# The ternary forms of the third window's gate and up move from VectorE to GpSimd, the opening begins in another order, and the third window's pairs are added in two steps

## The chip, the cores and the metric

One core of a Trainium2 chip runs the kernel. Its engines are TensorE (PE; PEld is its weight load), VectorE (DVE), ScalarE (ACT), GpSimd (POOL) and SyncE (SP), which issues most DMAs. The metric is the device time of one execution in microseconds (us), lower is better.

## The reference, cut to what matters

A batch of 32 sequences of 64 channels by 1024 features is first mixed over its channels (64x64 weights picked by an index of each sequence), then goes through a feed-forward layer whose weights are octonions quantized to -1, 0, 1 times a scale, and is added to the input.

```python
def ternary_dequant(W):
    scale = jnp.mean(jnp.abs(W))
    return scale * jnp.clip(jnp.round(W / scale), -1.0, 1.0)

def oct_ternary_linear(xp, W):          # xp: (..., 8, d)
    M = jnp.einsum('jik,jod->koid', S_OCT, ternary_dequant(W))
    return jnp.einsum('...id,koid->...ko', xp, M)

y = jnp.einsum('bct,bcd->bdt', x, cond_w[itok])
gate = oct_ternary_linear(y, w_gate); up = oct_ternary_linear(y, w_up)   # 8 x 341 hidden
h = silu(gate) * up
out = x + oct_ternary_linear(h, w_down)
```

## The kernel before, in words

The 2048 tokens are worked on in 8 tiles (T = 0 to 7) of 256. The 341 hidden rows of each octonion part are cut into three windows: two of 128 rows and a last one, "the third", of 85 (`THIRD`, `LAST`). In each tile 12 chunks c follow one another, four to a window; a chunk gives two of the eight parts of h. Chunks 0 to 7 belong to the two full windows, 8 to 11 to the third. A "down" stage ends the tile: `h` and sums of `h` (six rounds k = 0 to 5 of `z`, two to a window) are multiplied by the down weights.

Each engine has its own program, written out by hand; engines meet only at semaphores, and an engine runs its instructions in the order in which they are written. For a chunk PE makes sums in PSUM from the weight tables (`shared_pair`, `shared`, `own`), DVE adds the shared part, ACT takes the silu, DVE multiplies, ACT copies the result twice (`split_h`), DVE writes the low half (`h_lo`). PE may begin `own` of chunk c only when `h_lo` of chunk c - 2 is done.

**The opening.** Before the first product the weights' mean magnitudes must be known: ACT sums magnitudes (`sum_abs`), PE adds them over the partitions, DVE makes scale and half scale of them (`scales(m)`, m = 0 gate, 1 up, 2 down). DVE then makes the ternary form of a window in two instructions, a comparison at L919 and a comparison minus the first at L921 (`ternary`), and builds half of the table from it (`build_table`, four sums at L895); ACT copies or negates the rest (`copy_slots`). The activations y come as high and low half: `y_hi` on ACT, `y_lo` on DVE, in three pieces. PE starts chunk 0 when two pieces of `y_lo` are there, and its up half when the up table is.

**Tile 0.** Only window 0 of gate and up is made in the opening, and window 1 of gate. The rest stands between the chunks of tile 0 on DVE: `TERN_AFTER` and `TABLE_AFTER` say after which chunk a ternary form or a table (matrix, window) comes, `DOWN_AFTER` the same for the three windows of the down weights. After chunk 5 DVE makes the scales of tile 1 (`scales_of_tile(1)`). After chunk 6's `own`, PE begins to mix the down weights of the third (`mix`, L1201), which waits for the down weights' last ternary form and for the first of those scales. On GpSimd the sums of y (`sum_y(0)`) come first, then the mixing of the down weights' two full windows (`mix_down_weights`), and then five of the six rounds of z.

**A round of z** (`round_of_z`, GpSimd) waits for the four chunks of its window, adds pairs of h (`pair_up`, two or four instructions), and then adds and subtracts the pairs (two instructions). ACT writes the high half (`z_hi`), DVE the low half (`z_lo`). Round 5 is DVE's own (`last_round_of_z`). In the last tile ACT and DVE take round 5 before round 4:

```python
def last_rounds(T):
    ks = range(NR - 2, NR)
    return ks if T + 1 < NT else ks[::-1]
```

## Time and profile before

| | |
|---|---|
| median of 3 runs | 679.83 us (679.83 to 680.08) |
| the profiled execution | 679.09 us, its span 677.3 us |
| PE busy | 643.8 us (95% of the span) |
| PEld busy | 595.5 us (88%) |
| DVE busy | 516.5 us (76%) |
| POOL busy | 385.1 us (57%) |
| ACT busy | 323.2 us (48%) |
| mean TensorE clock granted | 0.986 |

Shares are of the whole span; the opening and tile 0 (the first 122 us) and the last tile look unlike the six tiles between. A matmul's end is modelled, so a PE that is shown busy can still be slow; its clock stands in a column of its own.

### The profile page before, as it was taken

How to read it: one execution, taken by the hardware profiler on the slowest of the kernel's cores; microseconds unless marked ns; L12 is line 12 of the kernel's file. 1: busy time of each engine (PE TensorE's matmuls, PEld its weight loads, DVE VectorE, ACT ScalarE, POOL GpSimd, SP SyncE). 2: the span in 40 equal slices, each digit the busy share in tenths (PEclk: the TensorE clock that was granted, in tenths of full speed). 3: DMA queues.
4: the chain of work that ended last, by engine and by line, in shares of the span. 5: the costliest groups of instructions: out<-in, count | busy, mean ns of one | idle time of the engine just before them, and what ended most of it. 6: DMA issues, size and time to landing. Idle time of an engine off the chain costs nothing. (4 is left out here: it accounts for less than half of the span.)

```text
span 677.3 us, 17118 instructions
## 1 busy us (share of the span) xinstructions
PE 643.8 (95%) x7010; PEld 595.5 (88%) x7010; DVE 516.5 (76%) x873; ACT 323.2 (48%) x542; POOL 385.1 (57%) x453
## 2 busy tenths in 40 slices
PE   3599899999999999999999999999999999999997
PEld 3378699899999999998998999999999999988986
DVE  1899977868776787868877698767878687787785
ACT  4847455345534545254454446254462545434440
POOL 1256685547637576348646476376754486465553
PEclk9799899999999999999999999999999999999997
DMA  9200030140003200041001300031000300021001
GB/s 345 67 2 1 1 116 15 39 155 1 2 2 102 90 2 2 1 137 55 2 2 61 132 1 2 1 126 68 1 2 6 121 1 2 2 72 55 2 1 63
DMA packets 10576, 31.50 MB, mean 47 GB/s; under 512 B 3330, under 2 KB 3330, under 8 KB 10370
## 3 DMA queue, kind: packets, MB, share of 16 engines
q1 hardware_dynamic: 9906, 28.81, 12.3%
q10 hardware_dynamic: 592, 1.61, 0.7%
q8 instruction: 55, 0.90, 0.6%
q14 instruction: 23, 0.19, 0.1%
HBM read 22.02 MB, written 8.39 MB: 45 GB/s over the span
## 5 line engine op out<-in xcount | busy, mean ns | idle before, releaser
L1240 PE MATMUL ps<-y_op,gate_table 128*128 128x256 f16 x1408 | 182.6, 275 | 8.2 <-DVE y_op L979 4.2
L1240 PE MATMUL ps<-y_op,up_table 128*128 128x256 f16 x1408 | 180.3, 273 | 0.2 <-ACT up_table L724 0.2
L1240 PEld LDWEIGHTS ps<-y_op,gate_table 128*128 128x128 f16 x1408 | 138.3, 99 | 27.3 <-issue 4.4
L1240 PEld LDWEIGHTS ps<-y_op,up_table 128*128 128x128 f16 x1408 | 137.9, 98 | 16.8 <-DVE up_table L895 0.7
L617 POOL TENSOR_TENSOR h_pairs<-h_f 128x256 f32<-128x256 f32 (+2 forms) x128 | 118.0, 949 | 60.0 <-ACT h_f L767 57.7
L524 POOL TENSOR_TENSOR o_sb<-o_sb,wd_sb 128x256 f32<-128x256 f32 (+1 forms) x150 | 87.4, 617 | 90.8 <-DVE wd_sb L1108 89.6
L617 POOL TENSOR_TENSOR z_f<-h_pairs 128x512 f32<-128x512 f32 (+1 forms) x80 | 103.7, 1317 | 43.0 <-DVE z_op L995 41.2
L1248 PE MATMUL ps<-third_table,y_op 128*128 128x170 f16 x1408 | 108.2, 237 | 0.6 <-ACT third_table L724 0.6
L1248 PEld LDWEIGHTS ps<-third_table,y_op 128*128 128x128 f16 x1408 | 105.1, 97 | 1.1 <-issue 0.8
L822 ACT ACTIVATE ps<-ps,small 128x512 f32<-128x512 f32 x64 | 42.4, 662 | 111.0 <-DVE ps L1009 85.0
L1401 PE MATMUL ps<-down_u,z_op 128*128 128x256 f16 (+1 forms) x768 | 92.8, 277 | 2.0 <-DVE z_op L995 2.0
L1401 PE MATMUL ps<-down_c,h_op 128*128 128x128 f16 (+1 forms) x1536 | 92.8, 220 | 0.0
L895 DVE TENSOR_TENSOR pu_sb<-ps,q_sb 128x170 f32<-128x170 f32 (+1 forms) x128 | 64.9, 507 | 33.9 <-PE ps L1240 14.1
L1401 PEld LDWEIGHTS ps<-down_c,h_op 128*128 128x128 f16 (+1 forms) x1536 | 89.6, 98 | 0.7
L1401 PEld LDWEIGHTS ps<-down_u,z_op 128*128 128x128 f16 (+1 forms) x768 | 75.0, 99 | 11.4 <-DVE z_op L995 2.1
L988 DVE TENSOR_TENSOR h_op<-ps,h_op 128x512 f16<-128x512 f32 (+1 forms) x96 | 65.8, 685 | 21.8 <-ACT h_f L767 21.8
L995 DVE TENSOR_TENSOR z_op<-z_f,z_op 128x1024 f16<-128x1024 f32 (+1 forms) x40 | 49.5, 1237 | 34.1 <-ACT z_op L782 34.1
L762 ACT ACTIVATE h_op<-ps 128x512 f16<-128x512 f32 (+1 forms) x96 | 57.3, 597 | 31.4 <-DVE ps L1083 30.6
L767 ACT ACTIVATE h_f<-ps 128x512 f32<-128x512 f32 (+1 forms) x96 | 57.6, 600 | 0.0
L782 ACT ACTIVATE z_op<-z_f 128x1024 f16<-128x1024 f32 (+1 forms) x40 | 42.1, 1053 | 32.2 <-POOL z_f L617 32.2
L1083 DVE SCALAR_TENSOR_TENSOR ps<-pu_sb,small,ps 128x512 f32<-128x512 f32 x64 | 48.3, 755 | 8.1 <-ACT ps L822 2.0
L1009 DVE TENSOR_TENSOR pu_sb<-ps,pu_sb 128x512 f32<-128x512 f32 x48 | 32.9, 686 | 19.4 <-PE ps L1240 19.4
(98 smaller groups left out, 643.2 us busy)
## 6 DMA issues: line engine op xcount, KB each, us to landing
x_in<-in_x_dram SPq DMA_DIRECT2D x8, 1024.0 KB, 5.1
o_sb<-in_x_dram SPq DMA_DIRECT2D x16, 512.0 KB, 3.7
out_dram<-o_sb SPq DMA_DIRECT2D x15, 512.0 KB, 2.7
h_op<-in_L_ffn_w_gate_dram ACTq DMA_DIRECT2D x3, 512.0 KB, 6.8
h_op<-in_L_ffn_w_up_dram SPq DMA_DIRECT2D x3, 512.0 KB, 7.4
z_op<-in_L_ffn_w_down_dram SPq DMA_DIRECT2D x1, 1536.0 KB, 11.4
out_dram<-o_sb SPq DMA_DIRECT2D x2, 256.0 KB, 2.2
cond_bd<-in_L_cond_weights_dram SPq DMA_DIRECT2D x30, 16.0 KB, 3.0
```

The source lines that it names most:

```text
L524: last = eng.tensor_tensor(dst, dst, wd_sb[:, s, k1, r0, h, :], ALU.add if sign > 0 else ALU.subtract)
L617: return pool.tensor_tensor(dst, a, b, ALU.add if sign > 0 else ALU.subtract)
L762: act.activation(h_op[rows, c, :, 0, :], h_bank(c), ACT.Copy).then_inc(h_hi_ready, 1)
L767: act.activation(h_f[rows, c], h_bank(c), ACT.Copy).then_inc(h_copied, 1)
L822: act.activation(bank_r(s, 0), bank_r(s, 0), ACT.Silu, scale=gate_scale(T)).then_inc(silu_ready, 1)
L895: return dve.tensor_tensor(dst, a, b, ALU.add if sign > 0 else ALU.subtract)
L988: dve.tensor_tensor(h_op[rows, c, :, 1, :], h_bank(c), h_op[rows, c, :, 0, :], ALU.subtract).then_inc(h_lo_ready, 1)
L995: dve.tensor_tensor(z_op[rows, k, 1], z_of(k), z_op[rows, k, 0], ALU.subtract).then_inc(z_lo_ready, 1)
L1083: dve.scalar_tensor_tensor(out=bank_r(s, 0), in0=u_sb[:], scalar=up_scale(T), in1=bank_r(s, 0), op0=ALU.mult, op1=ALU.mult).then_inc(h_rea ...
L1240: mm = pe.matmul(dst, table[m][:, slot, q, :], y_op[:, op, e, :], start=(i == 0 and e == 0), stop=(i == len(terms) - 1 and e == 1))
L1248: mm = pe.matmul(dst, y_op[:, op, e, P * s:P * s + P], third_table[:, slot].rearrange("p m r -> p (m r)"), start=(i == 0 and e == 0), stop ...
L1401: mm = pe.matmul(banks[bank][:, place], operand[:, P * s:P * s + P], weights, start=(bank not in begun), stop=(last and i == ends[bank]), ...
```

## The change: what it does

Three edits. **The opening**: PE adds the gate's magnitudes after the first of the four rounds of y instead of after the second; DVE sums the magnitudes of two of up's windows instead of one, before the scales of y instead of after them; ACT sums one window instead of two, and copies its half of the up table before it sums the down weights; DVE's `h_scales(0)` moves behind the third piece of `y_lo`. **The third's ternary forms**: GpSimd makes them, in three instructions each (two comparisons and a subtraction, 128 x 8 x 85 elements), after the up table of window 0 is built and before it mixes the down weights; the readers wait for a semaphore of GpSimd's. DVE no longer makes them, and builds the third's gate table after chunk 4 instead of 5. **The third's pairs**: in every tile round 4 adds the pairs of chunks 8 and 9 as soon as these are there, those of chunks 10 and 11 later.

The diff, cut to its core:

```diff
-    TERN_AFTER = {1: (1, 1), 4: (0, 2), 6: (1, 2)}
-    TABLE_AFTER = {0: (0, 1), 2: (1, 1), 5: (0, 2), 6: (1, 2)}
+    TERN_AFTER = {1: (1, 1)}
+    TABLE_AFTER = {0: (0, 1), 2: (1, 1), 4: (0, 2), 6: (1, 2)}
...
+        def wait_for_tern(engine, m, w):
+
+            if w == THIRD:
+                engine.wait_ge(third_tern_ready, m + 1)
+            else:
+                engine.wait_ge(tern_ready[m], w + 1)
...
-        def pair_up(add, k, pairs):
+        def pair_up(add, k, pairs, parts=(0, 1)):
...
-                a_runs = [(slice(0, 2), signs[0])] if signs[0] == signs[1] else [
-                    (slice(a, a + 1), signs[a]) for a in range(2)]
+                a_runs = [(slice(0, 2), signs[0])] if signs[0] == signs[1] and len(parts) == 2 else [
+                    (slice(a, a + 1), signs[a]) for a in parts]
...
+            def ternary_of_third(m):
+                raw_at, dst = [ap[m][THIRD][:, :, 0:LAST] for ap in (raw, tern)]
+                above = pairs_of_down[:, 0:2].rearrange("p n j o -> p (n j) o")[:, :, 0:LAST]
+                pool.wait_ge(scale_ready, 3 * (m + 1))
+                if m > 0:
+                    pool.wait_ge(third_tern_ready, m)
+                pool.tensor_scalar(above, raw_at, half[m], None, ALU.is_gt).then_inc(third_compared, 1)
+                pool.tensor_scalar(dst, raw_at, minus_half[m], None, ALU.is_lt).then_inc(third_compared, 1)
+                pool.wait_ge(third_compared, 2 * m + 2)
+                pool.tensor_tensor(dst, above, dst, ALU.subtract).then_inc(third_tern_ready, 1)
...
             def round_of_z(T, k):
                 n = (NR - 1) * T + k
-                pool.wait_ge(h_copied, NC * T + 4 * (k // 2) + 4)
-                if n > 0:
+                if k == NR - 2:
+
+                    pool.wait_ge(h_copied, NC * T + NC - 2)
                     pool.wait_ge(z_ready, n)
-                pair_up(signed_add, k, h_pairs).then_inc(pairs_ready, 1)
+                    pair_up(signed_add, k, h_pairs, (0,))
+                    pool.wait_ge(h_copied, NC * T + NC)
+                    pair_up(signed_add, k, h_pairs, (1,)).then_inc(pairs_ready, 1)
...
                 if T == 0:
+
+                    pool.wait_ge(slots_built[1], NBUILD)
+                    ternary_of_third(0)
+                    ternary_of_third(1)
                     mix_down_weights(0)
                     mix_down_weights(1)
...
-            for w in range(NQ - 1):
-                sum_abs_of(1, w)
+            sum_abs_of(1, 0)
             y_hi(0)
+            copy_slots(1, 0)
             act.wait_ge(down_loaded, 16)
-            sum_abs(2 * NQ - 1, raw_down_at, NQ * raw_n, abs_sum[2])
-            copy_slots(1, 0)
+            sum_abs(NQ + 1, raw_down_at, NQ * raw_n, abs_sum[2])
...
             build_table(0, 0)
+            for w in range(1, NQ):
+                dve.wait_ge(up_loaded[w], 16)
+                dve.tensor_reduce(abs_sum[1][:, w:w + 1], raw[1][w].rearrange("p j o -> p (j o)"), AX.X, ALU.add,
+                                  apply_absolute_value=True).then_inc(abs_summed_dve, 1)
             y_scales(0)
...
             scales_of_ffn()
-            h_scales(0)
             y_lo(0, range(2))
             ternary_of(1, 0)
             build_table(1, 0)
             y_lo(0, range(2, NY))
+            h_scales(0)
             ternary_of(0, 1)
...
-            for r in range(2):
-                y_round(0, r)
+            y_round(0, 0)
             sum_abs(0)
-            for r in range(2, 4):
+            for r in range(1, 4):
                 y_round(0, r)
             row_norms(0)
```

How the instructions stand now. First DVE in the opening, from the last piece of the gate table (before: from the last scale of y) to the first pieces of `y_lo`; L1123 (after: L1156) is the sum of magnitudes, L945 to L954 (L978 to L987) the scales of y, L901 and L905 (L934, L938) `scales(1)`, L959 to L967 `h_scales(0)`. Before:

```order
L954 TENSOR_SCALAR small<-small 128x1
L1123 TENSOR_REDUCE small<-h_op 128x1
L901 TENSOR_REDUCE small<-ps 128x1
L905 TENSOR_SCALAR small<-small 128x1 x3
L909 TENSOR_SCALAR small<-small 128x1
L911 TENSOR_SCALAR small<-small 128x1
L959 TENSOR_SCALAR small<-small 128x1
L962 TENSOR_SCALAR small<-small 128x1
L965 RECIPROCAL small<-small 128x1
L967 TENSOR_SCALAR small<-small 128x1
L979 SCALAR_TENSOR_TENSOR y_op<-y_f,small,y_op 128x4x256 x2
```

After:

```order
L928 TENSOR_TENSOR gate_table<-z_op 128x2x128 x2
L1156 TENSOR_REDUCE small<-h_op 128x1 x2
L978 TENSOR_REDUCE small<-ps 128x1
L980 TENSOR_SCALAR small<-small 128x1
L983 TENSOR_SCALAR small<-small 128x1
L986 RECIPROCAL small<-small 128x1
L987 TENSOR_SCALAR small<-small 128x1
L934 TENSOR_REDUCE small<-ps 128x1
L938 TENSOR_SCALAR small<-small 128x1 x3
L942 TENSOR_SCALAR small<-small 128x1
L944 TENSOR_SCALAR small<-small 128x1
L1012 SCALAR_TENSOR_TENSOR y_op<-y_f,small,y_op 128x4x256 x2
```

The two sums now stand ahead of the scales of y, and the four instructions of `h_scales(0)` are gone from here.

Second GpSimd between `sum_y(0)` and the mixing of the down weights (`wd_sb<-o_sb` are that mixing's pairs). Before:

```order
L617 TENSOR_TENSOR y_f<-y_f 128x256 x2
L617 TENSOR_TENSOR y_f<-y_f 128x512
L617 TENSOR_TENSOR y_f<-y_f 128x256 x2
L617 TENSOR_TENSOR wd_sb<-o_sb 128x512 x2
L617 TENSOR_TENSOR wd_sb<-o_sb 128x384
```

After:

```order
L626 TENSOR_TENSOR y_f<-y_f 128x256 x2
L661 TENSOR_SCALAR wd_sb<-h_op,small 128x8x85
L662 TENSOR_SCALAR z_op<-h_op,small 128x8x85
L664 TENSOR_TENSOR z_op<-wd_sb,z_op 128x8x85
L661 TENSOR_SCALAR wd_sb<-h_op,small 128x8x85
L662 TENSOR_SCALAR z_op<-h_op,small 128x8x85
L664 TENSOR_TENSOR z_op<-wd_sb,z_op 128x8x85
L626 TENSOR_TENSOR wd_sb<-o_sb 128x512 x2
L626 TENSOR_TENSOR wd_sb<-o_sb 128x384
```

Six instructions of 680 elements a partition have come in.

Third DVE from the end of chunk 4 to the down weights' last ternary form (`o_sb<-z_op`). Before:

```order
L1083 SCALAR_TENSOR_TENSOR ps<-pu_sb,small,ps 128x512
L919 TENSOR_SCALAR z_op<-h_op,small 128x8x85
L921 SCALAR_TENSOR_TENSOR z_op<-h_op,small,z_op 128x8x85
L895 TENSOR_TENSOR pu_sb<-ps,q_sb 128x512
L988 TENSOR_TENSOR h_op<-ps,h_op 128x2x256
L895 TENSOR_TENSOR ps<-ps,pu_sb 128x256 x2
L895 TENSOR_TENSOR pu_sb<-ps,pu_sb 128x256 x2
L1083 SCALAR_TENSOR_TENSOR ps<-pu_sb,small,ps 128x512
L895 TENSOR_TENSOR third_table<-z_op 128x4x85 x2
L895 TENSOR_TENSOR third_table<-z_op 128x2x85 x2
L919 TENSOR_SCALAR o_sb<-z_op,small 128x1024
L921 SCALAR_TENSOR_TENSOR o_sb<-z_op,small,o_sb 128x1024
```

After:

```order
L1116 SCALAR_TENSOR_TENSOR ps<-pu_sb,small,ps 128x512
L928 TENSOR_TENSOR third_table<-z_op 128x4x85 x2
L928 TENSOR_TENSOR third_table<-z_op 128x2x85 x2
L928 TENSOR_TENSOR pu_sb<-ps,q_sb 128x512
L1021 TENSOR_TENSOR h_op<-ps,h_op 128x2x256
L928 TENSOR_TENSOR ps<-ps,pu_sb 128x256 x2
L928 TENSOR_TENSOR pu_sb<-ps,pu_sb 128x256 x2
L1116 SCALAR_TENSOR_TENSOR ps<-pu_sb,small,ps 128x512
L952 TENSOR_SCALAR o_sb<-z_op,small 128x1024
L954 SCALAR_TENSOR_TENSOR o_sb<-z_op,small,o_sb 128x1024
```

The gate's two ternary instructions of the third are gone, and its table stands where they stood, so that chunk 5 is followed at once by the down weights' ternary form.

## Rows read from the trace of the kernel before

**Rows 1.** The page: TensorE's busy time, share of the span, instructions

```profile
PE 643.8 (95%) x7010; PEld 595.5 (88%) x7010; DVE 516.5 (76%) x873; ACT 323.2 (48%) x542; POOL 385.1 (57%) x453
```

**Rows 2.** Busy time by stretch: stretch, its length, each engine's, PEclk, DMA share, GB/s

```profile
202.00:640.00 438.00, 437.01 (x4781) 406.31 (x4779) 336.65 (x567) 205.59 (x337) 259.46 (x306) 1.00 0.12 41
```

**Rows 3.** PE's timeline: start, us busy, instructions [idle before <-releaser]

```profile
27.18 3.60 PE L1240 MATMUL ps<-y_op,gate_table 128*128 128x256 f16 x16 [4.21 <-DVE y_op L979]
...
69.86 1.91 PE L1240 MATMUL ps<-y_op,up_table 128*128 128x256 f16 x16
74.48 0.33 PE L1201 MATMUL ps<-o_sb,ident 128*128 128x128 f16 x3 [2.71 <-DVE small L945]
...
661.48 6.38 PE L1401 MATMUL ps<-down_u,z_op 85*128 85x256 f16 x32 [1.95 <-DVE z_op L995]
```

**Rows 4.** DVE's timeline, opening and chunk 0

```profile
20.23 0.42 DVE L945 TENSOR_REDUCE small<-ps 128x1 f32<-128x256 f32 x1 [1.35 <-PE ps L1234]
...
21.26 1.21 DVE L1123 TENSOR_REDUCE small<-h_op 128x1 f32<-128x1024 f32 x1
...
24.65 2.47 DVE L979 SCALAR_TENSOR_TENSOR y_op<-y_f,small,y_op 128x1024 f16<-128x1024 f32 x2
...
30.22 1.81 DVE L979 SCALAR_TENSOR_TENSOR y_op<-y_f,small,y_op 128x1536 f16<-128x1536 f32 x1
31.95 0.75 DVE L919 TENSOR_SCALAR z_op<-h_op,small 128x1024 f16<-128x1024 f32 x1
32.73 1.28 DVE L921 SCALAR_TENSOR_TENSOR z_op<-h_op,small,z_op 128x1024 f16<-128x1024 f32 x1
34.77 0.69 DVE L895 TENSOR_TENSOR pu_sb<-ps,q_sb 128x512 f32<-128x512 f32 x1 [0.76 <-PE ps L1240]
...
38.28 1.15 DVE L895 TENSOR_TENSOR gate_table<-z_op 128x512 f16<-128x512 f16 x4
...
41.33 0.68 DVE L895 TENSOR_TENSOR pu_sb<-ps,q_sb 128x512 f32<-128x512 f32 x1
```

**Rows 5.** DVE's timeline, chunks 5 to 7 of tile 0

```profile
68.09 2.57 DVE L895 TENSOR_TENSOR third_table<-z_op 128x340 f16<-128x340 f16 x4
...
80.72 0.90 DVE L895 TENSOR_TENSOR third_table<-z_op 128x340 f16<-128x340 f16 x4
81.54 1.22 DVE L995 TENSOR_TENSOR z_op<-z_f,z_op 128x1024 f16<-128x1024 f32 x1
```

**Rows 6.** ACT's timeline: first pieces of y, round 0 of z, round 5 of tile 7

```profile
21.37 2.19 ACT L746 ACTIVATE y_op<-y_f,small 128x1024 f16<-128x1024 f32 x2
...
79.78 1.06 ACT L782 ACTIVATE z_op<-z_f 128x1024 f16<-128x1024 f32 x1
...
656.74 1.06 ACT L782 ACTIVATE z_op<-h_f 85x1024 f16<-85x1024 f32 x1 [4.82 <-DVE h_f L895]
```

**Rows 7.** POOL's groups by shape up to 130 us: busy, mean ns | idle before

```profile
L617 POOL TENSOR_TENSOR wd_sb<-o_sb 128x512 f16<-128x512 f16 x4 | 4.5, 1154 | 24.1 <-DVE o_sb L921 24.1
...
L669 POOL TENSOR_SCALAR down_u<-down_u 128x256 f16<-128x256 f16 x2 | 1.7, 850 | 0.2
```

**Rows 8.** POOL's groups by shape, 130 to 640 us

```profile
L617 POOL TENSOR_TENSOR z_f<-h_pairs 128x512 f32<-128x512 f32 x54 | 67.4, 1269 | 31.3 <-DVE z_op L995 30.2
...
L617 POOL TENSOR_TENSOR h_pairs<-h_f 128x256 f32<-128x256 f32 x56 | 38.9, 725 | 33.0 <-ACT h_f L767 33.0
```

**Rows 9.** POOL's and DVE's timelines, end of tile 7

```profile
652.00 4.16 POOL L617 TENSOR_TENSOR h_pairs<-h_f 85x256 f32<-85x256 f32 x4 [3.10 <-ACT h_f L767]
656.24 2.83 POOL L617 TENSOR_TENSOR z_f<-h_pairs 85x512 f32<-85x512 f32 x2
...
657.83 2.32 DVE L995 TENSOR_TENSOR z_op<-h_f,z_op 85x1024 f16<-85x1024 f32 x1 [1.12 <-ACT z_op L782]
660.20 1.22 DVE L995 TENSOR_TENSOR z_op<-z_f,z_op 85x1024 f16<-85x1024 f32 x1
```

**Rows 10.** TensorE's clock around the last wait: stretch, length, PE busy, PEclk, DMA, GB/s

```profile
662.00:664.00 2.00, 2.00 (x12) 0.54 0.03 8
```

More of the change, by code:

```diff
@@ L405, in build @@
         fixed_scales = sem("fixed_scales")
+        third_compared = sem("third_compared")
+        third_tern_ready = sem("third_tern_ready")
         compared = sem("compared")
@@ L648, in mix_down_weights @@
                 pool.wait_ge(tern_ready[2], w + 1)
+                if w == 0:
+                    pool.wait_ge(third_tern_ready, 2)
                 if w > 0:
@@ L673, in round_of_z @@
                 n = (NR - 1) * T + k
-                pool.wait_ge(h_copied, NC * T + 4 * (k // 2) + 4)
-                if n > 0:
+                if k == NR - 2:
+                    pool.wait_ge(h_copied, NC * T + NC - 2)
                     pool.wait_ge(z_ready, n)
-                pair_up(signed_add, k, h_pairs).then_inc(pairs_ready, 1)
+                    pair_up(signed_add, k, h_pairs, (0,))
+                    pool.wait_ge(h_copied, NC * T + NC)
+                    pair_up(signed_add, k, h_pairs, (1,)).then_inc(pairs_ready, 1)
+                else:
+                    pool.wait_ge(h_copied, NC * T + 4 * (k // 2) + 4)
+                    if n > 0:
+                        pool.wait_ge(z_ready, n)
+                    pair_up(signed_add, k, h_pairs).then_inc(pairs_ready, 1)
                 pool.wait_ge(pairs_ready, n + 1)
@@ L757, in split_h @@
                 if T == 0 and c % 4 == 0:
-                    act.wait_ge(tern_ready[0], c // 4 + 1)
-                    act.wait_ge(tern_ready[1], c // 4 + 1)
+                    wait_for_tern(act, 0, c // 4)
+                    wait_for_tern(act, 1, c // 4)
                 rows = slice(0, ROWS[c // 4])
@@ L1120, in _ @@
             build_table(0, 0)
+            for w in range(1, NQ):
+                dve.wait_ge(up_loaded[w], 16)
+                dve.tensor_reduce(abs_sum[1][:, w:w + 1], raw[1][w].rearrange("p j o -> p (j o)"), AX.X, ALU.add,
+                                  apply_absolute_value=True).then_inc(abs_summed_dve, 1)
             y_scales(0)
-            dve.wait_ge(up_loaded[NQ - 1], 16)
-            dve.tensor_reduce(abs_sum[1][:, NQ - 1:NQ], raw[1][NQ - 1].rearrange("p j o -> p (j o)"), AX.X, ALU.add,
-                              apply_absolute_value=True).then_inc(abs_summed_dve, 1)
             scales(1)
             scales_of_ffn()
-            h_scales(0)
             y_lo(0, range(2))
@@ L1184, in sum_abs @@
             def sum_abs(m):
-                pe.wait_ge(abs_summed, (NQ, 2 * NQ - 1, 2 * NQ)[m])
                 if m == 1:
-                    pe.wait_ge(abs_summed_dve, 1)
+                    pe.wait_ge(abs_summed_dve, NQ - 1)
+                pe.wait_ge(abs_summed, NQ + m)
                 pe.matmul(totals(m), ones[:], abs_sum[m], start=True, stop=True).then_inc(totals_ready, 1)
```

4 lines of the change are left out of this document (2 added, 2 removed).

## The prediction

> **What bounds the kernel now.** I began with the page and the busy time by stretch: PE is busy for 643.8 of 677.3 us [rows 1], and from 202 to 640 us for 437.01 of 438 at full clock [rows 2]. The reader is to see that the six middle tiles have nothing to give: whatever DVE, ACT and POOL do there lies under matmuls. So only the opening, tile 0 and the end of the last tile can move the time. PE's timeline shows where it waits there [rows 3]: 4.21 us before the first product, for `y_lo` on DVE; 2.71 us at 71.77 to 74.48 before the mixing, for a scale of tile 1 that DVE comes to late; 1.95 us before 661.48, for round 4 of z. In between, DVE's timeline is nearly gapless from 27 us to the end of chunk 7: tile 0 goes at DVE's pace, and PE's waits there are what DVE leaves. I therefore follow DVE's queue.
>
> **A price that decides: DVE against GpSimd.** The four table sums of the third take 2.57 us at 68.09, while POOL works, and 0.90 at 80.72, while it is idle [rows 5]. At the end of tile 7 the row says it outright [rows 9]: DVE's `z_lo` starts at 657.83 and takes 2.32 us, the next one 1.22. POOL's last z instruction ends at 656.24 + 2.83 = 659.07, and 659.07 + 1.22 = 660.29, which is within 0.15 us of the slow one's end. So a DVE instruction of this kind doesn't run slower beside POOL, it waits until POOL's instruction is over, and POOL waits in turn. I take that for the comparisons, for table sums and for `y_lo`; the chunk's own additions, which read PSUM, are 0.68 to 0.69 us wherever they stand [rows 4] and I let them run free.
>
> **What POOL's new instructions cost.** Six of 680 elements a partition. Two-input f32 instructions give 725 ns for 256 and 1269 for 512 elements [rows 8]: 2.13 ns an element and 0.18 us fixed. The subtraction is f16; 512 elements are 1154 ns [rows 7], so (1154 - 180)/512 = 1.9 ns an element, 1.47 us for 680. For a comparison the nearest row is the one scalar operation, 850 ns for 256 [rows 7]: with 0.18 fixed, 2.62 ns an element, 1.96 us. The bounds: 0.9 us, if one input costs half of two an element (0.18 + 680 x 1.06 ns); 2.26 us, if the 850 ns are all slope. I take 1.96, by the row of its own kind. The sum is 4 x 1.96 + 2 x 1.47 = 10.8 us.
>
> **The opening.** DVE waits 1.35 us for the norms before 20.23 [rows 4], and the earlier sum on PE starts its queue about 1.5 us earlier, since it no longer stands behind the second round of y. Two sums of 1.21 us [rows 4] fit in, and the scales of y still begin at 20.2. Up's scale then needs no sum behind them, `h_scales(0)` is gone from before `y_lo`, and the first piece of `y_lo` waits only for ACT's first piece, at 21.37 + 1.1 = 22.5 [rows 6], where it began at 24.65 [rows 4]. That is 2.15 us gained; PE's first product comes at 25.0, and the up table, since ACT no longer sums the down weights first, 2.15 us earlier too.
>
> **Then POOL comes in.** The table of up's window 0 is ready at 28.15, and the third piece of `y_lo` (1.81 us) holds DVE to 29.88. POOL's first comparison runs 29.9 to 31.8. DVE has done `h_scales` by 30.6 and waits for it; its comparison (0.75) 31.8 to 32.6; POOL's second to 34.6; DVE's second ternary instruction (1.28) to 35.85, where chunk 0 starts (all three durations in [rows 4]). It started at 34.77: the 2.15 us are lost and 1.1 more. Chunk 0 is free of POOL (3.5 us with the down scales, 34.77 to 38.28), while POOL does its third and fourth, 35.85 to 39.4. The table of gate's window 1 asks at 39.4; POOL's fifth holds to 41.3, one sum of four, POOL's sixth to 43.2, three sums to 44.0. The down weights' ternary form takes 2.0 (38.28 + 1.15 = 39.4 to 41.33 before), so chunk 1 begins at 46.0 instead of 41.33 [rows 4]: **4.7 us late**. PE is idle from about 39.5 to 47 and will fall to the low clock; it has slack enough to be level with DVE again by chunk 4.
>
> **What comes back in tile 0.** After chunk 4 the gate's table of the third stands where its ternary form stood, about as long, so chunk 5 stays 4.7 late. Behind chunk 5 the 2.50 us of that table (68.09 to 70.59 [rows 5]) are gone, and the next ternary form meets a little less of POOL: chunk 6 is 2.0 late. PE ends `own` of chunk 6 at 71.77 + 4.7 = 76.45 and the scale is there at about 76.4: the wait of 2.71 us is gone, but PE then waits about 1 us for `h_lo` of chunk 5 instead, so PE follows DVE here too. After chunk 6 up's ternary form, which ended at 80.7 [rows 5], is gone; the table is followed by `z_lo` of round 0, which needs ACT's high half: 79.78 + 1.06 + 2.0 = 82.85 [rows 6] against 81.54 before [rows 5]: 1.3 late, 1.6 if POOL's pairs of round 1 hold up the table. From there on every engine is shifted alike. **Tile 0: +4.7 - 3.3 = +1.4 us.** What DVE is spared is 3.8 us of queue; it pays 6.85 us of waiting for POOL in the opening.
>
> **The pairs in two steps.** In tiles 0 to 6 they lie under PE [rows 2]; without that cover they would be worth up to the last tile's amount each. In tile 7 POOL has two of four additions (4.16 us [rows 9]) done before 652.0. It finishes z at about 657.0 instead of 659.07. But its long z instructions now fall between the four of DVE's round 5, which shift from 656.7 to about 658.0, and ACT takes round 5 first (656.74 [rows 6], then 658.0). Round 5's high half to 659.1, round 4's to 660.1, the two low halves to 661.5; before it was 660.20 + 1.22 = 661.42. **+0.1 us**; bounds -1.1 (round 5 stays at 656.74) and +0.3.
>
> The sum: 679.09 + 1.4 + 0.1 = 680.6 us for an execution like the profiled one. The median of the runs lies 0.74 above that one, so I predict **681.3**.
>
> **Weighed against the skill.** The row says 2.62 ns an element for a scalar operation on POOL [rows 7]. [...] The skill's "Perfetto Trace Analysis", section "Optimizing Scalar/DVE Operations", warns that moving work between GpSimd and DVE may not help, as they share a port; the 2.32 us of [rows 9] agree.
>
> **Rivals.** (1) *Cheap comparisons: faster.* At 0.9 us each POOL's turns are 30.8, 32.4, 35.2, 36.2, 37.1, 38.7; DVE waits 0.15, 0.9 and 1.4 us, chunk 1 starts at 41.8, tile 0 ends at +0.5 - 3.3 = -2.8: 677.1. If the blocking hardly bound at all, it would be down to -5: 675. It decides below 1.6 us for a comparison, where a straight line from -2.8 (0.9 us) to +1.4 (1.96 us) crosses zero. For it: a one-input read. Against it: the 850 ns. (2) *The end pays.* If DVE slips its round 5 between POOL's instructions, `z_lo` ends 1.1 us earlier; and if the shorter wait keeps the clock, which is granted at 0.54 from 662 us on [rows 10], the 32 matmuls of 6.38 us [rows 3] save up to 3.2 more: 680.2 down to 677. Against it: DVE's and POOL's turns add up whatever their order. (3) *Dearer turns.* At 2.26 us or above, or with each of the four table sums behind a turn of its own, chunk 1 is 6 to 7.5 us late: 683 to 685. That the opening's 2.15 us don't come is no case of its own: chunk 0 would then meet the same turns, later.
>
> **How the numbers follow.** The likeliest case, 680 to 683, 0.52; rival 1 0.25, rival 2 0.11, rival 3 0.12. A measurement here tells 0.2% (1.36 us) from no change. Faster (below 678.5): most of rival 1, half of rival 2, 0.27. Same: the lower part of the likeliest and what is left of these two, 0.31. Slower: 0.42. Below 677 there is about 0.1, above 684 about as much: the range is 677 to 684.
>
> **What would show it.** In the profile after: DVE's first `y_lo` near 22.5; POOL's comparisons near 1.96 us; comparisons of 1.5 us and more on DVE between 30 and 36; chunk 1's first addition near 46; PE without a wait before the mixing, the third's first product 1 to 2 us late; the last wait of PE near 1.9 us still. I am wrong if the comparisons cost below 1.6 us, if DVE's instructions aren't held for whole turns, or if PE's wait at the end has gone.

## The result: 673.61 us, faster, and the prediction was wrong

The changed kernel takes 673.61 us (median of 5 executions, 673.3 to 674.72), the one before 679.83 on the same chip (5 executions, 677.98 to 680.16). The ratio is 0.9923, with a 95% interval of 0.9908 to 0.9939. I had said 681.3, with a range of 677 to 684. The profiled execution took 673.46 us; its span is 671.5 us against 677.3, so 5.8 us are to be found.

First the page of the kernel after: busy time, share of the span and instructions, as in [rows 1].

```profile
PE 642.1 (96%) x7010; PEld 595.1 (89%) x7010; DVE 523.7 (78%) x870; ACT 322.1 (48%) x540; POOL 394.7 (59%) x459
```

DVE has lost instructions and is busy for 7.2 us more; POOL has six more and is busy for 9.6 us more. Neither says anything of the time.

PE's timeline after (start, us busy, instructions, in brackets the idle time before and what ended it) answers to [rows 3]:

```profile
24.41 3.59 PE L1274 MATMUL ps<-y_op,gate_table 128*128 128x256 f16 x16 [4.60 <-DVE y_op L1012]
...
70.49 0.33 PE L1235 MATMUL ps<-o_sb,ident 128*128 128x128 f16 x3
72.98 1.92 PE L1274 MATMUL ps<-y_op,gate_table 128*128 128x256 f16 x16 [0.56 <-DVE h_op L1021]
...
78.85 3.71 PE L1282 MATMUL ps<-third_table,y_op 128*128 128x170 f16 x48 [1.30 <-ACT third_table L758]
87.06 0.27 PE L1235 MATMUL ps<-o_sb,ident 128*128 128x128 f16 x2 [0.65 <-ACT down_u L871]
...
654.35 7.01 PE L1435 MATMUL ps<-down_u,z_op 85*128 85x256 f16 x32 [2.09 <-DVE z_op L1028]
661.15 6.87 PE L1435 MATMUL ps<-down_c,h_op 128*128 128x128 f16 x96
```

The first product comes 2.77 us earlier. The mixing of the third starts without its wait of 2.71 us, 3.99 us earlier, and the last mixing of tile 0 (87.06) stood at 91.95 before, 4.89 us later. The wait at the end is still there, and the 32 matmuls behind it take 7.01 instead of 6.38 us.

The two groups of DVE and POOL on which the prediction stands. DVE's timeline after, opening and chunk 0, against [rows 4]:

```profile
27.45 1.81 DVE L1012 SCALAR_TENSOR_TENSOR y_op<-y_f,small,y_op 128x1536 f16<-128x1536 f32 x1
...
30.00 0.74 DVE L952 TENSOR_SCALAR z_op<-h_op,small 128x1024 f16<-128x1024 f32 x1
30.78 1.28 DVE L954 SCALAR_TENSOR_TENSOR z_op<-h_op,small,z_op 128x1024 f16<-128x1024 f32 x1
...
35.90 1.60 DVE L928 TENSOR_TENSOR gate_table<-z_op 128x512 f16<-128x512 f16 x4
...
38.23 1.73 DVE L954 SCALAR_TENSOR_TENSOR o_sb<-z_op,small,o_sb 128x1024 f16<-128x1024 f32 x1
39.88 0.68 DVE L928 TENSOR_TENSOR pu_sb<-ps,q_sb 128x512 f32<-128x512 f32 x1
```

POOL's timeline after, over the same stretch:

```profile
27.64 3.71 POOL L661 TENSOR_SCALAR wd_sb<-h_op,small 128x680 f16<-128x680 f32 x1 [5.56 <-DVE up_table L928]
31.33 2.59 POOL L662 TENSOR_SCALAR z_op<-h_op,small 128x680 f16<-128x680 f32 x1
34.00 1.48 POOL L664 TENSOR_TENSOR z_op<-wd_sb,z_op 128x680 f16<-128x680 f16 x1
35.66 1.99 POOL L661 TENSOR_SCALAR wd_sb<-h_op,small 128x680 f16<-128x680 f32 x1 [0.17 <-DVE small L938]
37.62 2.42 POOL L662 TENSOR_SCALAR z_op<-h_op,small 128x680 f16<-128x680 f32 x1
40.13 1.48 POOL L664 TENSOR_TENSOR z_op<-wd_sb,z_op 128x680 f16<-128x680 f16 x1
```

The reader is to see whose row got longer. A comparison that isn't held up takes 1.99 us (35.66) and a subtraction 1.48; 1.96 and 1.47 were predicted. But POOL's first comparison takes 3.71 us: DVE's `y_lo` runs until 29.26, and the comparison ends 2.1 us after that. DVE's three instructions beside POOL's two comparisons take 1.81, 0.74 and 1.28 us, to 0.01 us what they took in [rows 4], although the last two begin while POOL's first comparison is under way. DVE pays in two places: 1.60 instead of 1.15 us for the table, 1.73 instead of 1.28 for the ternary form, begun 0.24 and 0.61 us after a comparison. That is 0.9 us in all, where I had counted 6.85. Chunk 1 starts at 39.88; I had said 46.0, and before it was 41.33.

**The ledger.** Some of the 2.77 us at the start is input that arrived earlier in this execution: the row norms' product on PE, which no edit speeds up by itself, comes at 18.34 against 19.15. Other executions of the changed kernel have it anywhere from 18.08 to 19.32. From that product on, in PE's timeline:

| stretch | before | after | difference |
|---|---|---|---|
| start to the row norms' product | 19.15 | 18.34 | -0.8 |
| to the last mixing of tile 0 (91.95; 87.06) | 72.80 | 68.72 | -4.1 |
| to the start of tile 7 (593.82; 586.55) | 501.87 | 499.49 | -2.4 |
| to the last matmul's start (673.61; 667.79) | 79.79 | 81.24 | +1.45 |

The sum is -5.8 us. So there are two gains, of 4.1 in the opening with tile 0 and of 2.4 in the seven boundaries between tiles, where I had said there was nothing to give, and a loss at the end.

### The profile page after: what moved, and what is told of

The parts are those of the page before. It is cut to its first block and busy times, and to the rows that moved or that the text cites. A ratio compares the mean times of both kernels' runs of the same rounds, so it can differ in the third digit from the quotient of the medians.

```text
span 671.5 us, 17121 instructions
## 1 busy us (share of the span) xinstructions
PE 642.1 (96%) x7010; PEld 595.1 (89%) x7010; DVE 523.7 (78%) x870; ACT 322.1 (48%) x540; POOL 394.7 (59%) x459
## 5 line engine op out<-in xcount | busy, mean ns | idle before, releaser
L626 POOL TENSOR_TENSOR h_pairs<-h_f 128x256 f32<-128x256 f32 (+2 forms) x128 | 112.5, 905 | 50.1 <-ACT h_f L801 46.7
L626 POOL TENSOR_TENSOR z_f<-h_pairs 128x512 f32<-128x512 f32 (+1 forms) x80 | 106.1, 1347 | 40.6 <-DVE z_op L1028 38.7
L928 DVE TENSOR_TENSOR pu_sb<-ps,q_sb 128x170 f32<-128x170 f32 (+1 forms) x128 | 64.8, 507 | 44.0 <-ACT q_sb L833 21.6
L1028 DVE TENSOR_TENSOR z_op<-z_f,z_op 128x1024 f16<-128x1024 f32 (+1 forms) x40 | 51.7, 1293 | 13.6 <-ACT z_op L816 13.6
L645 POOL TENSOR_TENSOR y_sq<-y_sq 128x512 bf16<-128x512 bf16 x12 | 13.9, 1154 | 60.0 <-ACT y_sq L768 60.0
(101 smaller groups left out, 677.4 us busy)
```

Source lines behind the costliest of these rows:

```text
L626: return pool.tensor_tensor(dst, a, b, ALU.add if sign > 0 else ALU.subtract)
L928: return dve.tensor_tensor(dst, a, b, ALU.add if sign > 0 else ALU.subtract)
L1028: dve.tensor_tensor(z_op[rows, k, 1], z_of(k), z_op[rows, k, 0], ALU.subtract).then_inc(z_lo_ready, 1)
```

## Experiments

"After the norms" below is a time counted from the row norms' product of the same execution, so that an early or late input doesn't count. Three batches were run, each with the kernel before on its own chip; ratios are to that.

Two profiles of one and the same code still differ after the norms. Six profiles have the changed kernel's opening and tile 0: in three of them chunk 1 starts 20.94 us and the last mixing 68.1 us after the norms, in the other three 21.5 to 21.6 and 68.7 to 68.8. Of the opening of the kernel before there are three profiles: two have 22.2 and 72.80, the third (the addition moved, below) has 23.06 and 73.66. PE's timeline of that third one shows where it starts; in [rows 3] stands the same gate half, and the up half behind it took 1.91 us:

```profile
29.89 2.58 PE L1240 MATMUL ps<-y_op,up_table 128*128 128x256 f16 x16 [0.24 <-ACT up_table L724]
```

The granted clock is 0.50 there until 31 us, and DVE's chunk 0 waits for it. So a difference of less than 0.9 us between two profiles, up to the end of tile 0, isn't shown to be an edit's.

### Each edit alone

The kernel before with one of the three edits put in. Opening alone:

```diff
+            for w in range(1, NQ):
+                dve.wait_ge(up_loaded[w], 16)
+                dve.tensor_reduce(abs_sum[1][:, w:w + 1], raw[1][w].rearrange("p j o -> p (j o)"), AX.X, ALU.add,
...
-            for r in range(2):
-                y_round(0, r)
+            y_round(0, 0)
```

> The kernel before with the new opening alone. Both theories let the first product come 2.7 us earlier, as in the changed kernel (24.4 instead of 27.2 us), since GpSimd has nothing new to do. Tile 0 goes at VectorE's pace, so chunk 1 should start about 2.3 us earlier (39.0 instead of 41.3 us), and nothing takes it back: about 677.4 us, ratio 0.9965. Against that stands that the wait before the mixing stays, and with it the time at the low clock. Should the opening alone give more than 3.5 us, my splitting by stage is wrong.

Third's ternary forms alone (`ternary_of_third`, `wait_for_tern`, `TERN_AFTER` and `TABLE_AFTER` as in the change):

> The kernel before with the third's ternary forms on GpSimd alone. Theory A (a comparison with a scalar on GpSimd holds VectorE for about 0.45 us of its 2, a two-input instruction for all of it): chunk 1 starts at most 1.5 us later than 41.3, the wait of 2.7 us before the mixing goes, tile 0 ends 2 to 4 us earlier: 675.8 to 677.8. Theory B (the prediction's: VectorE waits for whole comparisons): chunk 1 starts 4 us or more later, at 45 or beyond, and the kernel is at 679.5 to 682.

Pairs alone:

```diff
+                    pair_up(signed_add, k, h_pairs, (0,))
+                    pool.wait_ge(h_copied, NC * T + NC)
+                    pair_up(signed_add, k, h_pairs, (1,)).then_inc(pairs_ready, 1)
```

> The kernel before with the pairs in two steps alone. Theory A (TensorE waited about 0.35 us at each of 7 tile boundaries for VectorE's first sums of the down stage, which the trace calls issue; with the pairs earlier VectorE is there in time): a tile takes 78.19 instead of 78.54 us, 2.4 us in all, less 0 to 1.4 us for the low clock at the end: 677.4 to 679. Theory B (the prediction's: it all lies under TensorE): tiles stay at 78.54 and the time within 0.3 us of before, 679.5 to 680.2.

| kernel | median us | ratio, 95% | last mixing after the norms | a tile |
|---|---|---|---|---|
| before (this batch) | 679.17 | | 72.80 (profile of before) | 78.54 |
| opening alone | 677.54 | 0.9974 (0.9965 to 0.9982) | 71.68 | 78.56 |
| third alone | 675.93 | 0.9955 (0.9939 to 0.997) | 70.63 | 78.54 |
| pairs alone | 675.69 | 0.995 (0.9934 to 0.9966) | 72.80 | 78.19 |

Each edit gains by itself. By these profiles the opening is worth 1.1 us up to the last mixing and the third 2.2, together they gave 4.1. The 0.8 us left over don't show that the two help each other: measured from the other profile of the old opening (73.66) they are worth 2.0 and 3.0, and together 4.9. The pairs leave tile 0 as it was and shorten every tile by 0.35 us, 2.4 us over seven boundaries. The first two medians are as the first theory had them (677.4; 675.8 to 677.8). That of the pairs lies lower than the expected 677.4 to 679, 3.5 us below before; where the other 1.1 us come from stands under "The end, and the clock". DVE's timeline of the third alone, where POOL's six instructions meet DVE in the old order:

```profile
30.45 0.75 DVE L945 TENSOR_SCALAR z_op<-h_op,small 128x1024 f16<-128x1024 f32 x1
31.23 1.65 DVE L947 SCALAR_TENSOR_TENSOR z_op<-h_op,small,z_op 128x1024 f16<-128x1024 f32 x1
...
37.37 1.16 DVE L921 TENSOR_TENSOR gate_table<-z_op 128x512 f16<-128x512 f16 x4
38.45 0.77 DVE L945 TENSOR_SCALAR o_sb<-z_op,small 128x1024 f16<-128x1024 f32 x1
39.26 1.73 DVE L947 SCALAR_TENSOR_TENSOR o_sb<-z_op,small,o_sb 128x1024 f16<-128x1024 f32 x1
40.91 0.68 DVE L921 TENSOR_TENSOR pu_sb<-ps,q_sb 128x512 f32<-128x512 f32 x1
```

Again no DVE instruction is held for a turn: 1.65 and 1.73 instead of 1.28, and nothing else. Chunk 1 does start 1.3 us later after the norms than before (40.91 against norms at 17.45). The second of these rows is 0.45 of it; the first lies in front of a wait for PE. The rest goes with the low clock that PE still had in its first up half (16 matmuls in 2.50 us; 1.91 before), as in the profile with 2.58 above, which has nothing new on POOL and starts chunk 1 0.9 later. And yet tile 0 ends 2.2 us earlier: what DVE is spared later is worth 3.4.

### What a POOL instruction takes from DVE, by kind

The opening alone, with instructions on POOL whose results nobody reads, in the place of the new ones: four comparisons of 680 elements, or five additions of two inputs, about 10 us of either.

```diff
+                    for i in range(4):
+                        if i > 0:
+                            pool.wait_ge(filler_done, i)
+                        pool.tensor_scalar(filled, raw_at, half[0], None, ALU.is_gt).then_inc(filler_done, 1)
```

> The new opening alone (as e1_opening) and, before the mixing of the down weights, four comparisons with a scalar on GpSimd, 680 elements each, whose results nobody reads: about 8 us of GpSimd between 27.5 and 36 us. Theory A (such an instruction holds VectorE only for its first 0.45 us or so): VectorE's ternary form and chunk 0 between 29 and 35 us are as in e1_opening to within 0.5 us, chunk 1 starts at most 1 us later than there. Theory B (it holds VectorE for its whole 2 us): chunk 1 starts 3 to 5 us later.

> The same with five additions of two tensors on GpSimd, 680 elements each (1.6 us each, 8 us in all, results unread). Theory A (only two-input instructions hold VectorE for all their time) and theory B agree on a delay here: the comparison after the third piece of y_lo and the one behind it wait about 1 to 1.6 us each, chunk 1 starts 2 to 5 us later than in e1_opening. If it starts within 1 us of it, neither kind holds VectorE for long, and the 2.32 us of the end of tile 7 had another cause.

Measured: 679.72 us, ratio 1.0003 (0.9993 to 1.0013), with comparisons, 679.94 us, 1.0008 (0.9998 to 1.0018), with additions, in a batch whose kernel before took 678.96. That is no difference between the two kinds that can be told, and both lie about 2 us above the opening alone of another batch, of which chunk 1 explains less than half; the rest I can't place (the length of the end, which differs between executions of one kernel, is a candidate). What tells the kinds apart is the trace. POOL and DVE, timelines, beside comparisons:

```profile
28.46 10.44 POOL L702 TENSOR_SCALAR wd_sb<-h_op,small 128x680 f16<-128x680 f32 x4 [5.56 <-DVE up_table L903]
```
```profile
30.82 0.75 DVE L927 TENSOR_SCALAR z_op<-h_op,small 128x1024 f16<-128x1024 f32 x1
31.60 1.29 DVE L929 SCALAR_TENSOR_TENSOR z_op<-h_op,small,z_op 128x1024 f16<-128x1024 f32 x1
...
37.29 1.47 DVE L903 TENSOR_TENSOR gate_table<-z_op 128x512 f16<-128x512 f16 x4
```

Beside additions:

```profile
27.96 9.62 POOL L702 TENSOR_TENSOR wd_sb<-h_op 128x680 f16<-128x680 f32 x5 [5.54 <-DVE up_table L903]
```
```profile
30.34 0.99 DVE L927 TENSOR_SCALAR z_op<-h_op,small 128x1024 f16<-128x1024 f32 x1
31.37 2.22 DVE L929 SCALAR_TENSOR_TENSOR z_op<-h_op,small,z_op 128x1024 f16<-128x1024 f32 x1
...
37.01 1.58 DVE L903 TENSOR_TENSOR gate_table<-z_op 128x512 f16<-128x512 f16 x4
```

One ternary instruction of DVE (1.28 alone) takes 1.29 beside comparisons and 2.22 beside additions; there is one profile of each, but beside a comparison it took at most 1.74 in any other profile, the changed kernel's among them. So the kind of the POOL instruction matters, and the row from which I took the rule, `z_lo` in [rows 9], stands beside two-input additions. But additions don't do what I had forecast either: three DVE instructions pay 0.24, 0.94 and 0.43 us, 1.6 in all for 9.62 us of POOL, and of that chunk 0 gives back some, since DVE waited there for PE anyway (0.76 us in [rows 4]). Chunk 1 starts 21.79 us after the norms, against 21.09 with the opening alone and 21.50 with comparisons. It is 0.7 and 0.4 us, no more than two profiles of the same code differ by, where I had expected 2 to 5 us with additions and, rightly, at most 1 with comparisons.

That leaves the 2.32 us of `z_lo` itself. In the changed kernel POOL is done with its additions at 650.27, and the same `z_lo` at 651.94 takes 1.22 us; so the 1.1 us more are paid beside POOL, and they are of the size of the 0.94. Whether that one was held right to the end of POOL's instruction stays open.

The comparisons twice, in the changed kernel:

```diff
                 pool.tensor_scalar(above, raw_at, half[m], None, ALU.is_gt).then_inc(third_compared, 1)
+                pool.wait_ge(third_compared, 4 * m + 1)
+                pool.tensor_scalar(above, raw_at, half[m], None, ALU.is_gt).then_inc(third_compared, 1)
```

> The changed kernel, with each of GpSimd's four comparisons made twice over the same output (the second after the first), so that GpSimd has about 8 us more between 27 and 42 us; it computes the same. Theory of the prediction (a DVE instruction waits for the whole of a comparison): at least four more turns of 2 us in front of DVE, chunk 1 some 4 to 8 us later than 39.9, tile 0 several us longer, 676 to 679 us. Theory after the runs so far (scalar comparisons hold DVE by no more than 0.45 us each, and GpSimd waits for DVE instead): chunk 1 begins by 1.5 us later at most, counted from the row norms' product; GpSimd's mixing of the down weights begins some 8 us later than 41.75 and is hidden by its later wait of 4.3 us in part, the third's forms come before anything reads them; the time is that of the changed kernel within 1 us.

Measured: 678.08 us, ratio 0.9964 (0.9936 to 0.9991); the changed kernel took 674.21 on the same chip, the one before 680.06. On DVE the second theory held: chunk 1 starts 20.96 us after the norms, where profiles with half the comparisons have 20.94 to 21.62. On the time it missed: 3.9 us more, not within 1. ACT's, DVE's and PE's timelines of the kernel with doubled comparisons show where they went:

```profile
77.78 1.06 ACT L820 ACTIVATE z_op<-z_f 128x1024 f16<-128x1024 f32 x1 [3.64 <-POOL z_f L626]
...
80.10 0.72 ACT L762 ACTIVATE third_table<-third_table 128x255 f16<-128x255 f16 x2
```
```profile
78.87 1.37 DVE L1032 TENSOR_TENSOR z_op<-z_f,z_op 128x1024 f16<-128x1024 f32 x1 [3.46 <-ACT z_op L820]
```
```profile
81.07 6.29 PE L1286 MATMUL ps<-third_table,y_op 128*128 128x170 f16 x48 [5.05 <-ACT third_table L762]
```

POOL begins the mixing 9 us later (50.87 against 41.75) and round 0's sums still 4.8 us later; ACT waits 3.64 us for it, and the third's table stands behind that wait in ACT's queue; PE waits 5.05 us for the table, and falls to a slower clock behind it (48 matmuls in 6.29 us instead of 3.71). The last mixing of tile 0 is 72.88 us after the norms against 68.72. So work on POOL does have a price here, but the price is POOL's own lateness, not DVE's. In the changed kernel POOL ends round 0's sums at 70.44 + 2.49 = 72.93, and ACT comes to them at 75.56: 2.6 us of slack are left.

### The boundaries between tiles

DVE's timeline at the start of tile 2, of the kernel before:

```profile
202.89 2.06 DVE L1108 SCALAR_TENSOR_TENSOR wd_sb<-ps,small,ud_sb 128x512 f32<-128x512 f32 x3
206.59 0.69 DVE L895 TENSOR_TENSOR pu_sb<-ps,q_sb 128x512 f32<-128x512 f32 x1 [1.65 <-ACT q_sb L799]
```

and of the kernel after:

```profile
196.61 1.40 DVE L1141 SCALAR_TENSOR_TENSOR wd_sb<-ps,small,ud_sb 128x512 f32<-128x512 f32 x2
201.10 0.69 DVE L928 TENSOR_TENSOR pu_sb<-ps,q_sb 128x512 f32<-128x512 f32 x1 [3.09 <-ACT q_sb L833]
```

DVE ends the additions of the down stage (`add_down`) 1.4 us earlier before it waits for the new tile: round 4's pairs come in two steps, so round 4 of z is done earlier, and its `z_lo` and what follows it. The views of waits of PEld and of PE, 92 to 640 us (us in total, times, the longest), have this in the kernel before, one line each, and neither line in the kernel after:

```profile
PEld ps L1240 <- issue: 3.0, 7, 0.5
...
PE ps L1240 <- issue: 1.2, 6, 0.2
```

L1240 has the first products of a tile: seven waits of the weight load, six of the matmul, none over 0.5 us. "Issue" says that the profile found no releaser. My guess was DVE: the first product needs a bank that `add_down` of the first half frees. The test is the kernel before with that one addition moved ahead of the last piece of `y_lo`:

```diff
-                    y_lo(T + 1)
+                    y_lo(T + 1, range(2))
+                    add_down(T, 0)
+                    y_lo(T + 1, range(2, NY))
+                    add_down(T, 1)
```

> The kernel before, in which VectorE does the first half's sums of the down stage (add_down of s = 0) between the second and the third piece of y_lo instead of behind the third. If TensorE's 0.35 us at each tile boundary are a wait for these sums, which free its bank, a tile takes 78.19 instead of 78.54 us and the time falls by 2.4 us, as it did with the pairs in two steps: 677 to 677.5 us against 679.4. If they are a wait for anything else (y_lo, a fetch of code), tiles stay at 78.54.

Measured: 675.01 us, ratio 0.9937 (0.9922 to 0.9952). Every tile takes 78.19 us, as in the changed kernel, with GpSimd's order untouched and the last piece of `y_lo` even later; both lines of waits are gone. So the wait is for `add_down`, and this exchange on DVE's queue does in the steady tiles what the pairs do. The 4.0 us are more than the seven boundaries give and more than I had expected (677 to 677.5); the rest is at the end, as with the pairs (see there).

The reverse, the changed kernel without the pairs:

```diff
-                    pair_up(signed_add, k, h_pairs, (0,))
-                    pool.wait_ge(h_copied, NC * T + NC)
-                    pair_up(signed_add, k, h_pairs, (1,)).then_inc(pairs_ready, 1)
+                pair_up(signed_add, k, h_pairs).then_inc(pairs_ready, 1)
```

> The changed kernel with the pairs of the third back in one step. Theory of the prediction (pairs worth nothing in tiles 0 to 6): the same time as the changed kernel but for 0.1 us. Theory after the runs so far: each of the seven boundaries costs 0.35 us again (tiles of 78.54 us instead of 78.19), so 2.4 us more; at the end round 5 is again in front of round 4's additions, the last wait about 2 us. Whether the clock comes back after about 7 us or after 12 to 13 us decides another 1.3 us: 674.5 to 676 us in all. Opening and tile 0 as in the changed kernel: the mixing of the third ends 4 us earlier than before, counted from the row norms' product.

Measured: 675.5 us, 0.9941 (0.9928 to 0.9955), tiles of 78.58 us. The seven boundaries come back; counted from the norms to the last matmul it is 2.0 us above the changed kernel of the same batch (this profile's tile 0 is 0.7 shorter, see the spread above), in the medians 1.3. That is inside the 674.5 to 676 us expected, and not the same time, as the prediction would have it.

### The end, and the clock

The changed kernel, twice more:

> The changed kernel once more, on the chip of the other three, to compare them with it and to see its end a second time. In e3_pairs TensorE waited 1.81 us for round 4 of z and kept its clock (32 matmuls in 3.67 us); in the changed kernel it waited 2.09 us and took 7.01. If the fall hangs on small differences of phase, it may come out either way here, between 9 and 13.7 us from the wait's end to the last matmul; if it hangs on the code, it is 13.4 again. Time 672.5 to 674.5 us.

> The changed kernel a third time, beside the others of this batch: about 673.3 us, tiles of 78.19 us, and at the end a wait of about 2 us with 13.5 us from there to the last product, if the long stretch at the low clock belongs to this kernel; 12.1 us if it came by chance twice.

Measured: 673.19 us, 0.9906 (0.9884 to 0.9929), and 674.21 us, 0.9912 (0.9894 to 0.9931). The gain stands. TensorE's clock and busy time after the last wait, by stretch, in the first profile of the changed kernel (stretch, length, busy us and instructions of PE, PEld, DVE, ACT and POOL, granted clock, DMA share, GB/s):

```profile
652.00:654.00 2.00, 0.26 (x5) 0.08 (x2) 2.00 (x2) 0.85 (x1) 0.00 (x0) 0.92 0.00 0
654.00:656.00 2.00, 1.65 (x8) 1.20 (x9) 1.61 (x3) 0.00 (x0) 0.00 (x0) 0.50 0.04 8
...
662.00:664.00 2.00, 2.00 (x22) 2.00 (x21) 1.72 (x3) 0.08 (x1) 1.92 (x5) 0.52 0.00 0
664.00:666.00 2.00, 2.00 (x39) 2.00 (x37) 1.97 (x6) 0.00 (x0) 2.00 (x5) 1.00 0.01 4
```

PE has been idle for 2.09 us and the granted clock is 0.50 (1.2 of 2.4 GHz) from 654 to past 662. The 32 matmuls of 256 columns take 7.01 us instead of 3.67, and the 96 of 128 columns behind them 6.87 instead of 5.53 (the rows of the pairs alone, below, have the full clock). From the end of the wait to the last matmul's start it is 13.45 us; before it was 12.13. In the profiles of all the kernels run:

| wait before round 4's products | to the last matmul | kernels |
|---|---|---|
| none | 6.1 (80 matmuls for 128) | changed kernel, end filled |
| 1.81 | 8.81, clock stays at 1.00 | pairs alone |
| 1.94 to 2.22 | 12.1 | before, opening alone, third alone, addition moved, comparisons unread, doubled comparisons |
| 2.09 to 2.23 | 13.45 to 13.8 | changed kernel (three times), without pairs, additions unread |

Behind the wait of 1.81 us the clock stayed, behind each of the others it fell. Why the same wait is followed by 12.1 or by 13.5 I don't know: the changed kernel without pairs has the long form, the changed kernel with doubled comparisons the short one, so it isn't the pairs.

Nor does the length of the wait decide by itself. Before the mixing in tile 0, PE of the kernel before waits 2.71 us and the clock falls; with the addition moved it waits 2.70 at the same place, and the clock stays. The next 16 matmuls of the gate half, in PE's timeline of the kernel before and of the one with the addition moved:

```profile
77.32 2.49 PE L1240 MATMUL ps<-y_op,gate_table 128*128 128x256 f16 x16
```
```profile
76.74 1.92 PE L1240 MATMUL ps<-y_op,gate_table 128*128 128x256 f16 x16 [0.80 <-DVE h_op L988]
```

Executions of one kernel on one chip also differ, and stand in groups by their mean granted clock. The kernel before in the last batch: two at 0.991 took 677.9 to 678.1 us, four at 0.986 took 678.8 to 679.2, eight at 0.985 took 679.9 to 680.8 (a fifteenth, 687.7 at 0.944, stands apart). With the addition moved: four at 0.991 took 674.9 to 675.5, the profiled one, at 0.986, took 676.25. With the pairs alone: three at 0.991, the profiled one among them, took 674.9 to 675.2, three at 0.986 or 0.987 took 676.2 to 676.7. Two of the changed kernel's 17 executions (669.9 at 0.993, 671.3 at 0.991) lie below all the others (672.5 to 674.7, 0.987). I take the groups for ends with the clock kept, with the short form and with the long one; only the profiled executions have traces, so that isn't shown, and the table above tells of those alone. It fits the 1.1 and 1.5 us that the medians of the pairs alone and of the addition moved have over their 2.4 at the boundaries. PE of the kernel with the pairs alone, profiled:

```profile
658.36 3.67 PE L1409 MATMUL ps<-down_u,z_op 85*128 85x256 f16 x32 [1.81 <-DVE z_op L1003]
661.87 5.53 PE L1409 MATMUL ps<-down_c,h_op 128*128 128x128 f16 x96
```

What the low clock costs the kernel is less than what it costs PE. From the end of the wait to the end of the span it is 14.7 us with the pairs alone, 15.8 in the kernel before and 17.15 in the changed kernel: 1.1 us for the short form and 2.4 for the long one. At the last matmul it is 3.3 and 4.6, but where the clock stays, DVE's additions end last.

If the wait and the low clock are what the end costs, filling the wait must give them back. In the last tile of the changed kernel PE now does half of the corrections (48 matmuls, which need only `h`) before it waits for round 4:

```diff
+                corrections(0)
...
-                for h in range(2):
-                    for w in range(NQ):
...
+                corrections(1)
```

> The changed kernel, where TensorE does half of the last tile's corrections of its second half (48 matmuls, about 2.7 us) before it waits for round 4 of z, instead of after. If the clock fell because of the 2.1 us wait at 652.3 us, the wait and the low clock behind it (about 10 us at half speed) both go: 2.1 us and 4 to 5 us, together about 6 us, of which the adding on VectorE behind it may take some back: 667.5 to 670.5 us. If the clock falls there for another reason, 2 us at most: 671.5.

> The changed kernel with one half of the corrections of the last tile (48 products) moved in front of PE's wait for round 4 of z, a second time, beside the changed kernel on the same chip. If the gain is the low clock's: no wait at the end, the clock stays at its upper level, and 2.4 to 2.8 us less than the changed kernel of this batch, about 670.8 us. If the first run was luck: the same as the changed kernel within 0.7 us.

Measured: 670.96 us, 0.988 (0.9861 to 0.9899), and in a later batch 671.89 us, 0.9888 (0.9871 to 0.9905), beside the changed kernel's 674.21 on the same chip: 2.3 us faster than it. Expected were 667.5 to 670.5 us and, the second time, 2.4 to 2.8 us; both measured gains are a little smaller. PE of the first of these runs:

```profile
653.94 3.66 PE L1435 MATMUL ps<-down_u,z_op 85*128 85x256 f16 x32
657.43 2.85 PE L1435 MATMUL ps<-down_c,h_op 128*128 128x128 f16 x48
```

There is no wait, the clock stays, and PE's last matmul starts at 660.06. In the second run it starts 642.57 us after the norms (661.30 less 18.73), 6.9 us earlier than in the first profile of the changed kernel (649.45). Less than half of that reaches the end, since now DVE is what is waited for. Its last instruction with the end filled:

```profile
662.83 1.41 DVE L1126 SCALAR_TENSOR_TENSOR o_sb<-ps,small,o_sb 128x512 f32<-128x512 f32 x2
```

and in the changed kernel, where it still waits for PE:

```profile
668.15 0.75 DVE L1126 SCALAR_TENSOR_TENSOR o_sb<-ps,small,o_sb 128x512 f32<-128x512 f32 x1 [0.81 <-PE ps L1435]
```

This is the best version that was run.

## Why the prediction was wrong

**"A DVE instruction of this kind doesn't run slower beside POOL, it waits until POOL's instruction is over ... I take that for the comparisons".** This is the step that failed, the wait of 6.85 us that DVE was to have for POOL in the opening; the runs show 0.9 us in its place. Chunk 1 starts at 39.88 and not at 46.0; 0.8 of these 6.1 us are the earlier input, the other 5.3 hang on this step. The row behind it, 2.32 us for a `z_lo`, is true, and it showed DVE against a two-input addition. I carried it over to one-input comparisons, of which the trace had none beside DVE. The unread comparisons and additions show that the kinds differ (1.29 and 2.22 us for the same instruction), and also that even additions don't make turns that add up. With the comparisons doubled, chunk 1 starts no later either. I had also let POOL be served every time. In the profile it is POOL that waits: 3.71 and 2.59 us for comparisons of 1.99.

The Trainium skill, "SBUF — State Buffer", section "Who interferes with whom", calls the port pair that DVE and GpSimd share an exclusive lock, held for the whole instruction by whoever issued first. For POOL behind DVE the trace agrees (the comparison that meets `y_lo` ends 3.71 us after its start, 2.1 us after `y_lo`). For DVE behind a comparison it doesn't: the comparison at 37.62 runs to 40.04, and DVE's instruction begun at 38.23 is done at 39.96, 0.45 us longer than alone.

**"4 x 1.96 + 2 x 1.47 = 10.8 us" on POOL.** Right: where DVE doesn't hold them up they take 1.99 and 1.48. The price on which I had thought that the sign hangs (rival 1, "below 1.6 us for a comparison") didn't decide it. The rival's side remark, "if the blocking hardly bound at all", is the case that came; it had 675, and the kernel came below that too, by the boundaries.

**The opening, "2.15 us gained".** Near: the first product comes 1.96 us earlier after the norms. But by chunk 1 only 0.64 are left in the changed kernel and 1.1 in the opening alone. The first up half on PE, which chunk 0 waits for, took 2.29 and 2.78 us in these two profiles, at a granted clock of 0.50 for part of it, and 1.91 before; that is 0.4 and 0.9 us. In the changed kernel POOL's 0.9 come on top. `h_scales(0)`, moved behind the third piece, costs nothing in the opening alone: DVE still waits 0.82 us for PE behind it.

**"What comes back in tile 0", 3.3 us.** Right: from chunk 1 to the last mixing the changed kernel gains 4.08 - 0.64 = 3.44 us. As forecast, PE's wait before the mixing is gone.

**"In tiles 0 to 6 they lie under PE".** This is the second step that failed, by 2.4 us. PE's busy share in [rows 2] is 437.01 of 438 us, and I read it as nothing to give. A gap of 0.35 us in a tile of 78.54 is below half a per cent and hides in such a share, above all as the end of a matmul is modelled. A wait before each tile's first product was there to be found in the view of waits, as "issue"; that it is for DVE, only the run with the addition moved showed.

**The end, "+0.1 us".** The step itself was right to 0.1 us: round 5's high half starts 1.38 us later relative to tile 7 (1.3 forecast), and round 4's `z_lo` ends 0.14 later. The loss of 1.45 us is a low clock that lasts longer, and a kernel without the pairs has it too; what decides between its two lengths stays open. Rival 2 had the mechanism that could have paid (a shorter wait keeps the clock, up to 3.2 us); with the pairs alone it did in the profile, 3.3 us at the last matmul and 1.1 at the end of the span, in the changed kernel the wait was 2.09 and it did not.

Predicted were +1.4 for tile 0, nothing for the boundaries and +0.1 for the end; measured are -4.9 (of it 0.8 the input), -2.4 and +1.45. That is the whole difference of 7.3 us between the forecast span and the measured one.

## What to carry to other kernels

A contention seen in a row holds for the pair of kinds in that row; before it is carried over to another kind (one input instead of two, the other engine first), it deserves the weight of a bound, not of the likeliest value. Work moved to GpSimd is then limited by what stands behind it in GpSimd's own queue: ask when that is first waited for (here 2.6 us of slack were left, and 8 us more of comparisons cost 3.9). And a busy share near 100% doesn't say that a steady stage has nothing to give: compare the period of a tile with the sum of its matmuls, and read the short waits at its boundary.

## What the runs showed of the hardware

GpSimd's comparison, f32 to f16, 680 elements a partition: 1.99 us where nothing held it up, 3.71 us where it began behind a DVE instruction of 1.81. A DVE instruction begun inside such a comparison was longer by 0 to 0.46 us, the four table sums together by up to 0.56 (35.41 in the changed kernel's second run, 1.71 for 1.15). Beside two-input additions one was longer by up to 0.94, and round 5's `z_lo` by 1.1 ([rows 9]).

At the end, in the profiles, a wait of PE of 1.81 us left the clock at its upper level, eleven of 1.94 to 2.23 us were followed by the lower one, and then the same 128 matmuls took 12.1 or 13.5 to 13.8 us. In tile 0 a wait of 2.70 us left the clock up in one profile, and one of 2.71 us was followed by the lower level in another, so these are no threshold. The low clock at the end cost 1.1 or 2.4 us of the kernel's time. 48 independent matmuls moved in front of the wait took away both, and gained 2.3 us.
